# Sorted expert tiles of 128 rows in place of 256 in the last stage of a four-block network

## What is computed

```python
def _moe_forward(x, Wfc_s, bfc_s, Wproj_s, bproj_s, Wr, Wfc, bfc, Wproj, bproj):
    xf = x.reshape(N, C)                                # C = 128, hidden 512, 8 experts
    shared = new_gelu(xf @ Wfc_s + bfc_s) @ Wproj_s + bproj_s
    probs = jax.nn.softmax(xf @ Wr, axis=-1)
    topk_p, topk_i = jax.lax.top_k(probs, 2)
    topk_p = topk_p / jnp.sum(topk_p, axis=-1, keepdims=True)
    gate = zeros((N, 8)).at[arange(N)[:, None], topk_i].add(topk_p)
    for e in range(8):
        h = new_gelu(xf @ Wfc[e] + bfc[e]) @ Wproj[e] + bproj[e]
        routed = routed + h * gate[:, e:e + 1]
    return shared + routed
```

## Time and profile before

| | us |
|---|---|
| three timed runs | 5725.06, 5733.82, 5733.53 (median 5733.53) |
| the profiled execution | 5728.82 |
| its span | 5726.9 |
| TensorE busy in it | 5045.7 (88%) |
| DVE, ACT, GpSimd busy | 3496.7, 3202.9, 2338.6 |
| mean granted TensorE clock | 0.932 of full |

### The profile page before, as it was taken

One profiled execution on the slowest core, in us unless ns is written; L12 is line 12 of the kernel. 1 busy time (PEld: TensorE's weight loads), 2 busy tenths in 40 slices (PEclk: granted clock), 3 DMA queues, 4 the chain that ended last, 5 costly groups with the idle time before them and its releaser, 6 DMA issues. The chain is left out here.

```text
span 5726.9 us, 106114 instructions
## 1 busy us (share of the span) xinstructions
PE 5045.7 (88%) x38512; PEld 2614.0 (46%) x38524; DVE 3496.7 (61%) x5705; ACT 3202.9 (56%) x7251; POOL 2338.6 (41%) x1954
## 2 busy tenths in 40 slices
PE   6999879979895899999889999997746999987998
PEld 2444324434442466665346666534422222224895
DVE  5787522277783566665356666446747999965444
ACT  2666743447675466665246666524523788884454
POOL 3333100022211788885068888500153222300765
PEclk7999989979998899999989999998866999998999
DMA  3344211133331000000100000000213233312222
GB/s 106 110 113 113 66 36 50 44 98 109 108 99 34 7 7 7 5 7 5 71 8 7 7 7 7 5 0 3 83 43 107 81 92 90 92 53 74 68 75 79
DMA packets 302987, 311.31 MB, mean 54 GB/s; under 512 B 74255, under 2 KB 244638, under 8 KB 300962
## 3 DMA queue, kind: packets, MB, share of 16 engines
q1 hardware_dynamic: 291362, 284.21, 17.2%
q0 software_dynamic: 11136, 20.59, 1.3%
HBM read 172.16 MB, written 123.99 MB: 52 GB/s over the span
## 5 line engine op out<-in xcount | busy, mean ns | idle before, releaser
L806 ACT ACTIVATE a_prob<-a_PB 128x512 f32<-128x512 f32 x2304 | 1253.1, 597 | 456.1 <-PE a_PB L648 342.2
L696 PE MATMUL a_PO<-a_prob,a_V 128*32 128x256 f32 (+3 forms) x8192 | 715.7, 422 | 22.5 <-ACT a_cn L779 22.3
L960 DVE TENSOR_REDUCE a_blocks<-a_PA 128x8 f32<-128x1024 f32 x512 | 602.1, 1215 | 37.1 <-PE a_PA L648 34.7
L963 DVE TENSOR_REDUCE a_neg<-a_PA 128x2 f32<-128x1024 f32 x512 | 591.0, 1213 | 34.7 <-PE a_PA L661 34.6
L661 PE MATMUL a_PA<-a_KS,a_QS 48*128 48x512 bf16 (+3 forms) x3072 | 470.0, 345 | 110.6 <-DVE a_blocks L960 69.6
L2689 DVE TENSOR_REDUCE f1a_neg<-f1a_PA 128x2 f32<-128x384 f32 (+1 forms) x512 | 267.0, 522 | 487.3 <-PE f1a_PA L2491 486.8
L2619 POOL TENSOR_TENSOR f1a_prob<-f1a_prob,f1a_inv 128x384 f32<-128x384 f32 (+1 forms) x512 | 395.0, 774 | 281.4 <-DVE f1a_inv L2693 281.4
L678 PE MATMUL a_PB<-a_QS,a_KS 51*128 51x512 bf16 (+3 forms) x3072 | 448.4, 329 | 56.5 <-ACT a_prob L806 54.9
L2583 ACT ACTIVATE f1a_pt<-f1a_PT 128x512 f32<-128x512 f32 (+1 forms) x512 | 278.7, 544 | 347.6 <-PE f1a_PT L2500 343.9
L2576 ACT ACTIVATE f1a_prob<-f1a_PA,f1a_neg 128x192 f32<-128x192 f32 (+1 forms) x1024 | 406.1, 405 | 67.8 <-DVE f1a_neg L2689 67.8
L661 PEld LDWEIGHTS a_PA<-a_KS,a_QS 48*128 48x128 bf16 x3072 | 123.5, 94 | 634.4 <-DVE a_blocks L960 202.8
(11 more groups left out here) (457 smaller groups left out, 10185.8 us busy)
## 6 DMA issues: line engine op xcount, KB each, us to landing
a_spill<-a_qkp SPq DMA_DIRECT2D x96, 384.0 KB, 3.1
a_QS<-a_spill SPq DMA_DIRECT2D x384, 96.0 KB, 2.5
a_KS<-a_spill SPq DMA_DIRECT2D x384, 96.0 KB, 2.5
a_spill<-a_qkp SPq DMA_DIRECT2D x96, 256.0 KB, 3.1
a_raw<-a_cn SPq DMA_DIRECT2D x192, 72.0 KB
a_spill<-a_qkp SPq DMA_DIRECT2D x96, 128.0 KB, 3.0
tokens_out<-f_y SPq DMA_DIRECT2D x78, 128.0 KB
a_heads<-a_raw SPq DMA_DIRECT2D x32, 256.0 KB, 3.3
```

Of the source, the lines that this page charges most:

```text
L696: mm = nc.tensor.matmul(PO[32 * j:32 * j + 32, first:last], V[:, par, t, 8 * e + pr], prob[:, k % st.ring, e, c + first - q0:c + last - q0 ...
L806: nc.scalar.activation(prob[:, k % st.ring, e], PB[:, ring_b.slot(0, ("b", s, e))], ACT.Exp, scale=scale).then_inc(pb_used, 1)
L960: nc.vector.tensor_reduce(to, of, AX, ALU.max).then_inc(pa_used, 1)
L963: nc.vector.tensor_reduce(neg[:, t, pr], PA[:, bank:bank + 2], AX, ALU.max, negate=True).then_inc(pa_used, 1)
```

## The change

`TS` becomes 128: the number of tiles is 87 + 55 = 142. Each tile has one gather, one transpose, up products of 128 columns, four down products, gelus of 128 columns, a store of 64 KB, and weight copies `w1c` and `w2c` of its own, of the same size as before. The list of source rows needs 142 columns in place of 156. The ring holds 56 tiles of 128 rows. The mixing in the loop starts at tile 105 and takes a pair each 2.7 tiles. The offset `first` of the second part is added one step later, and the expert of a tile is found with part-relative tile numbers.

```diff
-TS = 256
+TS = P
...
-    HALF = [2 * n for n in tiles_of]
-    NH = 2 * NX
-    RING = 32
+    RING = 56
...
-        own = sb("own", [P, 640])
+        own = sb("own", [P, 704])
...
-        y = sb("y", [P, 2, 2, P])
-        xin = rows[:].rearrange("p (r k) n -> p r k n", k=2)
+        y = sb("y", [P, 2, P])
+        xin = rows[:, 0:RING]
...
-        mix_at = {tiles_of[0] + 9 + j * 27 // 20: j for j in range(first_pairs)}
+        mix_at = {tiles_of[0] + 18 + j * 27 // 10: j for j in range(first_pairs)}
...
             def turn(i):
-                pe.wait_ge(got[i % RING], 32 * (i // RING + 1))
+                pe.wait_ge(got[i % RING], 16 * (i // RING + 1))
...
-                for k in range(2):
-                    tr = nc.tensor.transpose(PT[:, 0, k * P:(k + 1) * P], xin[:, i % RING, k], net.ident[:])
-                tr.then_inc(x_turned, 1)
+                nc.tensor.transpose(PT[:, 0, 0:P], xin[:, i % RING], net.ident[:]).then_inc(x_turned, 1)
...
-                for m in range(2):
-                    for k in range(F4):
-                        mm = nc.tensor.matmul(PO[:, i % 2, m * P:(m + 1) * P], hid[:, i % 2, k, m * P:(m + 1) * P], w2c[:, i % 2, k * P:(k + 1) * P],
-                                              start=(k == 0), stop=(k == F4 - 1))
+                for k in range(F4):
+                    mm = nc.tensor.matmul(PO[:, i % 2, 0:P], hid[:, i % 2, k, 0:P], w2c[:, i % 2, k * P:(k + 1) * P],
+                                          start=(k == 0), stop=(k == F4 - 1))
...
-                for k in range(2):
-                    nc.gpsimd.indirect_dma_start(
-                        out=xin[:, i % RING, k], out_offset=None, in_=net.buf,
-                        in_offset=bass.IndirectOffsetOnAxis(ap=source[:, 2 * i + k:2 * i + k + 1], axis=0),
-                        bounds_check=TT * P - 1, oob_is_err=False).then_inc(got[i % RING], 16)
+                nc.gpsimd.indirect_dma_start(
+                    out=xin[:, i % RING], out_offset=None, in_=net.buf,
+                    in_offset=bass.IndirectOffsetOnAxis(ap=source[:, i:i + 1], axis=0),
+                    bounds_check=TT * P - 1, oob_is_err=False).then_inc(got[i % RING], 16)
...
-            link(nc.vector.tensor_tensor(base[:], base[:], first[:], ALU.add))
             link(nc.vector.tensor_tensor(tiles[:], base[:], tiles[:], ALU.subtract))
+            link(nc.vector.tensor_tensor(tiles[:], tiles[:], first[:], ALU.add))
...
-                nc.vector.tensor_tensor(y[:, i % 2], PO[:, i % 2, 0:TS].rearrange("p (k n) -> p k n", n=P),
-                                        w2c[:, i % 2, F4 * P:].unsqueeze(1).broadcast_to([P, 2, P]), ALU.add).then_inc(y_out, 1)
+                nc.vector.tensor_tensor(y[:, i % 2], PO[:, i % 2, 0:P], w2c[:, i % 2, F4 * P:], ALU.add).then_inc(y_out, 1)
...
-        net.xout = nc.dram_tensor("tokens_out", [78 * TS, P], F32, kind="Internal").ap()
+        net.xout = nc.dram_tensor("tokens_out", [142 * TS, P], F32, kind="Internal").ap()
```

More of the change, by code:

```diff
@@ L1802, in token_experts_phase @@
         lane, name_of = sb("lane", [P, 1]), sb("name_of", [P, TT])
-        in_tile = sb("in_tile", [P, 4, 4, HALF[0]])
-        found, empty = sb("found", [P, NH]), sb("empty", [P, NH])
-        source = sb("source", [P, NH], U32)
+        in_tile = sb("in_tile", [P, 4, 4, tiles_of[0]])
+        found, empty = sb("found", [P, NX]), sb("empty", [P, NX])
+        source = sb("source", [P, NX], U32)
         tiles = sb("tiles", [P, 2, E8])
@@ L1823, in token_experts_phase @@
         xT = sb("xT", [P, 2, TS])
-        y = sb("y", [P, 2, 2, P])
-        xin = rows[:].rearrange("p (r k) n -> p r k n", k=2)
+        y = sb("y", [P, 2, P])
+        xin = rows[:, 0:RING]
         token_rows = net.buf.rearrange("(p t) n -> p t n", p=P)
-        PI = PT[:, 1, P:P + NH]
+        PI = PT[:, 1, P:P + NX]
         lgT = hid[:, 1]
@@ L1885, in store @@
                 sp.wait_ge(y_out, t + 1)
-                sp.dma_start(net.xout[t * TS:(t + 1) * TS].rearrange("(k p) n -> p k n", p=P), y[:, t % 2]).then_inc(stored[t % 2], 16)
+                sp.dma_start(net.xout[t * TS:(t + 1) * TS], y[:, t % 2]).then_inc(stored[t % 2], 16)
             for i in range(NX):
@@ L1960, in name_rows @@
                 for j in range(4):
-                    mm = nc.tensor.matmul(PI[:, h * HALF[0]:h * HALF[0] + HALF[h]], at_row[:, q % 4, j], in_tile[:, q % 4, j, 0:HALF[h]],
+                    mm = nc.tensor.matmul(PI[:, h * tiles_of[0]:h * tiles_of[0] + tiles_of[h]], at_row[:, q % 4, j], in_tile[:, q % 4, j, 0:tiles_of[h]],
                                           start=(j == 0 and q in (0, MAPS0)), stop=(j == 3 and q in (MAPS0 - 1, len(MAPS) - 1)))
@@ L2222, in _ @@
             late_tiles = tile_in[:, :, starts[1]:]
-            link(nc.vector.tensor_scalar(late_tiles, late_tiles, -float(HALF[0]), None, ALU.add))
+            link(nc.vector.tensor_scalar(late_tiles, late_tiles, -float(tiles_of[0]), None, ALU.add))
             def one_hot(q):
@@ L2232, in one_hot @@
                     n = 4 * nb + j
-                    ins = nc.vector.tensor_scalar(in_tile[:, q % 4, j, 0:HALF[h]], kf[:, 1, 0:HALF[h]], tile_in[:, c, n:n + 1], name_of[:, n:n + 1],
+                    ins = nc.vector.tensor_scalar(in_tile[:, q % 4, j, 0:tiles_of[h]], kf[:, 1, 0:tiles_of[h]], tile_in[:, c, n:n + 1], name_of[:, n:n + 1],
                                                   ALU.is_equal, ALU.mult)
@@ L2237, in address @@
             def address(h):
-                of = slice(h * HALF[0], h * HALF[0] + HALF[h])
+                of = slice(h * tiles_of[0], h * tiles_of[0] + tiles_of[h])
                 dve.wait_ge(mapped, MAPS0 if h == 0 else len(MAPS))
@@ L2250, in _ @@
                 seen = own[0:1, 0:tiles_of[h] * E8].rearrange("p (t e) -> p t e", e=E8)
-                link(nc.vector.tensor_tensor(seen, kf[0:1, 1, of].unsqueeze(2).broadcast_to(shape), base[0:1, h].unsqueeze(1).broadcast_to(shape), ALU.is_ge))
+                link(nc.vector.tensor_tensor(seen, kf[0:1, 1, 0:tiles_of[h]].unsqueeze(2).broadcast_to(shape), base[0:1, h].unsqueeze(1).broadcast_to(shape), ALU.is_ge))
                 link(nc.vector.tensor_reduce(known[0:1, of], seen, AX, ALU.add))
```

## The result

The changed kernel takes 5787.09 us (median of 4 runs, 5784.73 to 5792.07), the kernel before 5732.61 (4 runs, 5725.06 to 5733.82): ratio 1.0099, 95% interval 1.0081 to 1.0116. 5785 us was forecast. The profiled execution of after took 5792.07 us, with a span of 5790.3 us. The first two views of it are busy time by stretch (us of PE, PEld, DVE, ACT and POOL with instructions, granted clock, DMA), and the chain of waits (start us, us).

The account below looks back on a forecast made before the run. TensorE alone bounds the expert loop before; ACT was to bound it after. Loop +46.5, ahead of it +1 and tail +6.2 make +53.7 us: 5782.5 against the profiled run, 5787 against the median, forecast 5785, range 5760 to 5835.

Parts of the forecast that it names:

- TensorE at 1.89 us a tile: Expert loop: 17 transposes and passes of 0.111 us a tile, 268 us for 142 tiles, a gain of 23 us alone.
- ACT at 2.40 us a tile: Expert loop: four gelus 1.145, gap 0.71, copy to next gelu 0.54 us; ACT becomes the bound, between 2.19 and 2.71.
- The 0.71 us gap stays: Expert loop: ACT's idle time from its last gelu's end to the weight copy's start stays 0.71 us in every tile.
- The sign that the prediction gave: Expert loop: ACT's idle time would be nearly all behind its own gelus, 0.7 us before each copy.
- Another sign: Expert loop: TensorE would be busy about 80% of the time, at clock 1.00.
- The loop: Expert loop from first gelu to its end: 341.7 us where it took 294.2, net +46.5 us with the earlier first gelu.
- Ahead of the loop, +1 us, and the first gelu 1 us earlier: Before the expert loop: longer DVE tile counts cost net +1 us (0 to 2); fewer up-product columns bring the gelu forward.
- The tail, +6.2 us: Behind the last share: six late pairs instead of four, gathers held by four buffers, +6.2 us, bounds 2.9 and 8.
- The sum: Whole kernel: 46.5 + 1 + 6.2 = +53.7 us.
- A: Expert loop: ACT is not the bound, TensorE's 1.89 us a tile decide, 72 us less, 5713 us; chance 0.06.
- B: Expert loop: TensorE's clock falls, a quarter of the tiles at the low level, +43 us, 5828 us; chance 0.07.
- C: Expert loop: waits between engines, DVE or gelus cost more; 2.6 us a tile gives 5813, 2.75 gives 5834; chance 0.15.

Follow-up runs that it names:

- three buffers: The changed kernel with three w1c weight buffers on ACT in place of two: 5721.38 us, ratio 0.9985 to the kernel before.
- the doses of 0.22 and 0.5 us a tile: Two runs of the changed kernel: three transposes a tile in place of one, 5791.01 us; one more 640-column DVE copy a tile, 5791.89 us.

## Why the prediction was right

- **TensorE at 1.89 us a tile.** Right, though the change never shows it: with three buffers it is 1.90.
- **ACT at 2.40 us a tile.** Right: 2.38. Four gelus were put at 1.145 us and take 1.12 to 1.13; one was put at 365 ns by a row of another stage (an exponential that also sums, so not quite the same kind) and has a mean of 363. The Trainium skill's 280 ns plus 0.833 ns a column (ScalarE: Activation LUTs, "What ACT_TABLE_LOAD costs") makes 387, and the 2.52 us a tile that would follow did not come; the measurement decides for the row.
- **The 0.71 us gap stays.** Right in size and effect, by carrying over what the trace of before showed. What fills it was only half known. The sign that the prediction gave, idle time put down to ACT's own gelus, did not come: the profile of after names TensorE's up products. They signal last on `e_up`, for which the copy waits too, but only for an older tile's count. With that wait kept and the load left out, the gap was 0.09 us. And the load was taken for one part of several, while it and its address are 0.62 of 0.71. Another sign, TensorE busy about 80% of the time, reads 94% in the profile, for the modelled ends told above.
- **The loop.** From the first gelu 341.7 us were forecast, 338.8 measured; 0.02 us a tile make 2.8 us. What was not foreseen are five longer steps of 2.65 to 2.77 us among 99, some 1.5 us. They come again at the same distances in the profile of the change run again (83.6, 138.6, 167.4 and 222.5 us behind the first), so they belong to the program and are not chance; their cause stays open.
- **Ahead of the loop, +1 us, and the first gelu 1 us earlier.** -0.2 in all, against 0 forecast: the first up product starts 0.6 us later in the stage, and the gelu follows it 0.8 us sooner.
- **The tail, +6.2 us.** +7.7. The mechanism was right, buffers of four pairs that hold the last gathers back. Mis-sized were the gathers: I let those of the last but one pair start 0.1 us behind the mix, and they start 5771.29 - 5770.53 = 0.76 us behind it; and the eight of them come 5781.06 - 5771.29 = 9.77 us apart from first to last, where seven steps of 1.31 make 9.17. From the last weigh to the end of the last add it is 2.87 us, where 2.6 was taken.
- **The sum.** +53.7 against +54.0 in the stage, and +52.5 in the change run again. That it comes so close is in part luck: up to the end of the loop the forecast is 3.1 us too high, in the tail 1.5 too low, and the 1.4 us of clock behind the loop, which only one of the two profiles has, and 0.5 at the very end make up for the rest.
- **The rivals.** A (TensorE decides) needed the gap to go; with the gap out of the way it was 5721 and 5724 us, where 5713 was worked out: the loop gives 65.7 us, and 72 had been taken, some half of the rest since the step was 2.38 and not 2.40. B: the granted clock was 0.50 up to about 5342.7 us, 3.9 us behind the first gelu, and 1.00 from 5343 us to the end of the loop. The Trainium skill's warning about thin products with waits between them (TensorE: Matmul & The Clock Gate, "Why this matters for your kernels") did not come true with pauses of 0.34 us. C: TensorE and DVE have slack; the doses of 0.22 and 0.5 us a tile left the step alone.

## What to carry to other kernels

A cut that nearly doubles the number of tiles halves for each of them only what grows with the tile. List for each engine what it does once per tile, waits and register loads too, and compare the sums: here TensorE's side of the loop gained 21 us (294.2 to 273.1), and ACT, busy 30 of 50 us before, became the bound through 0.7 us a tile that the profile shows as idle. A register load behind a wait for the engine's own last instruction stands bare; one more buffer, so that the wait is for an older one, hides it; that and two more pairs mixed in the loop turned a loss of 0.9% to 1.0% into a gain of 0.4%.

## What the runs showed of the hardware

- Loading a register from SBUF on ACT and making an address from it costs 0.62 us when it is issued behind a fresh wait: a gap of 0.71 us ahead of the copy with it and 0.09 without. With three buffers, four gelus still queued ahead of it, nothing of it shows: 0.8 us of idle time ahead of 126 copies.
- The name on idle time can be the wrong one: where a wait is on two semaphores and a load follows, the profile named the engine that had signalled last (64 us ahead of 88 copies), and taking away the load left 0.09 us of 0.71.
- Identical code ahead of the stage put its start between 5216.6 and 5230.4 us in the ten profiles, so differences of less than some 10 us between single executions were read within the stage.
